# Softmax halves scaled back to back on GpSimd, the second sums ahead of the residual on VectorE, row places in PSUM

## What is computed

```python
x = x + xattn(layernorm(x), ctx)     # q, k, v, o with low-rank additions
                                     # softmax over 73 keys + softmax over 4 keys, 16 heads
h = layernorm(x)
top_logits, top_idx = top_k(h @ gate_w, 2)
top_w = softmax(top_logits)
x = x + sum_e combine[e] * (silu(h @ w1[e]) @ w2[e])
```

## Time and profile before

| | us |
|---|---|
| median of 3 runs | 716.13 (714.78 to 716.4) |
| the profiled execution | 715.26 |
| its span, first to last instruction | 713.5 |
| busy: TensorE / VectorE / GpSimd / ScalarE | 639.0 / 519.7 / 483.3 / 446.3 |
| mean granted TensorE clock | 0.988 of 2.4 GHz |

### The profile page before, as it was taken

How to read it: one execution, slowest core, us unless ns; L and a number is a source line. 1 busy time by engine, 2 the same in 40 slices (tenths; PEclk the granted TensorE clock), 3 DMA queues, 4 the chain that set the end, 5 groups by cost and what they waited for, 6 DMA issues and landing times. The chain is left out here.

```text
span 713.5 us, 22010 instructions
## 1 busy us (share of the span) xinstructions
PE 639.0 (90%) x7612; PEld 528.3 (74%) x7613; DVE 519.7 (73%) x1226; ACT 446.3 (63%) x768; POOL 483.3 (68%) x577
## 2 busy tenths in 40 slices
PE   6627799999999999999999999979999999999871
PEld 2215587788788888788788778757888888888751
DVE  3964679988988998898898898986577644445431
ACT  1436787778778778778778877854464454454330
POOL 3024645878878877977877887875677676556744
PEclk9999899999999999999999999999999999999997
DMA  8921111112111121111211211203769989655630
GB/s 263 322 79 21 32 34 52 48 45 68 47 55 57 47 62 50 59 53 48 75 36 48 80 32 48 78 16 77 119 124 136 133 119 139 92 82 87 86 48 6
DMA packets 87259, 55.31 MB, mean 78 GB/s; under 512 B 60784, under 2 KB 81520, under 8 KB 87216
## 3 DMA queue, kind: packets, MB, share of 16 engines
q1 hardware_dynamic: 73840, 37.41, 22.2%
q0 software_dynamic: 13376, 17.33, 13.4%
HBM read 20.27 MB, written 24.85 MB: 63 GB/s over the span
## 5 line engine op out<-in xcount | busy, mean ns | idle before, releaser
L527 POOL DMA_INDIRECT out_x<-pt_s,token_of x71 | 113.0, 1592 | 23.4 <-issue 21.4
L782 DVE TENSOR_TENSOR wq_s<-wk_s,wq_s 128x512 f16<-128x512 f32 (+1 forms) x78 | 51.5, 664 | 78.6 <-ACT wq_s L603 78.5
L598 ACT ACTIVATE wk_s<-ps 128x512 f32<-128x512 f32 (+1 forms) x78 | 43.5, 557 | 102.9 <-PE ps L1600 99.0
L1600 PE MATMUL ps<-ffnw,wq_s 128*128 x852 | 100.1, 273 | 6.3 <-DVE wq_s L782 4.8
L1600 PE MATMUL ps<-q_s,ffnw 128*128 128x256 f16 (+1 forms) x936 | 103.3, 264 | 2.1 <-issue 1.6
L959 POOL TENSOR_TENSOR prob<-prob,mx 128x1168 f32<-128x1168 f32 x64 | 77.6, 1233 | 37.6 <-DVE mx L1401 37.5
L1600 PEld LDWEIGHTS ps<-q_s,ffnw 128*128 x936 | 86.0, 98 | 15.2 <-issue 4.6
L1600 PEld LDWEIGHTS ps<-ffnw,wq_s 128*128 128x128 f16 x852 | 81.7, 98 | 19.8 <-issue 9.8
L1600 PE MATMUL ps<-wo_s,ot_s 128*128 128x256 f16 x768 | 89.4, 273 | 2.8 <-DVE ot_s L1338 2.8
L1600 PE MATMUL ps<-xt_s,wq_s 128*128 128x256 f16 x768 | 89.9, 279 | 1.9 <-DVE xt_s L1338 1.9
L1600 PEld LDWEIGHTS ps<-xt_s,wq_s 128*128 128x128 f16 x768 | 76.5, 100 | 13.0 <-issue 1.9
(11 more groups left out here) (232 smaller groups left out, 1176.0 us busy)
## 6 DMA issues: line engine op xcount, KB each, us to landing
wstage<-in_ffn_w SPq DMA_DIRECT2D x16, 512.0 KB, 3.6
x_sb<-in_x SPq DMA_DIRECT2D x4, 1024.0 KB, 10.8
out_x<-x_sb SPq DMA_DIRECT2D x16, 256.0 KB, 2.2
rows_dram<-wstage SPq DMA_DIRECT2D x8, 264.0 KB
out_x<-pt_s,token_of POOLq DMA_INDIRECT x71
pt_s<-in_wq SPq DMA_DIRECT2D x2, 512.0 KB, 4.4
pt_s<-in_wo SPq DMA_DIRECT2D x2, 512.0 KB, 8.4
rows_dram<-row_words,slot_i POOLq DMA_INDIRECT x64, 2.5
```

The lines of the kernel that those rows point to most:

```text
L527: pool.indirect_dma_start(out_rows, bass.IndirectOffsetOnAxis(ap=token_of[:, j % UNROLL, c:c + 1], axis=0), y_sb[:, j % UNROLL, c, :], Non ...
L598: act.activation(h32[:, half, 0:2 * n], h_ps(t, j, half)[:, 0:2 * n], ACT.Silu, scale=1 / WSCALE).then_inc(silu_done, 1)
L782: dve.tensor_tensor(hs[:, j % 2, 1, 2 * half:2 * half + 2, 0:n], h32[:, half, 0:2 * n].rearrange("p (f n) -> p f n", f=2), hs[:, j % 2, 0, ...
L1600: last = pe.matmul(o, lhs(a, n), rhs(c, n), start=(i == 0), stop=(i == len(steps) - 1))
```

## The change

Three things, in the streams of two engines. On GpSimd `normalise(b, 1)` follows `normalise(b, 0)` at once; `rstd_2(b - 1)` comes behind it, and then both scatters (in batch 15 the order stays as it was; in batch 1 only `rstd_2` changes its place). On VectorE `sums(b, 1)` comes ahead of `residual(b - 1)`, in every batch that has a residual. And `place` is no longer a tile in SBUF but 16 columns of the PSUM bank in which TensorE has left the ranks; `place` is written there by one VectorE instruction and read by the next but one, `picked`.

```diff
-        place = sb("place", [P, TPB, EXPERTS], F32)
...
                 normalise(b, 0)
-                if routed and not last:
-                    scatter(b - 2, 0)
-                if not first and not last:
+                normalise(b, 1)
+                if not first:
                     rstd_2(b - 1)
-                normalise(b, 1)
-                if last:
-                    rstd_2(b - 1)
+                if routed:
                     scatter(b - 2, 0)
                 if routed and not last:
                     scatter(b - 2, 1)
...
-                c.step(dve.tensor_tensor(place[:], rank, next_row[:].unsqueeze(1).to_broadcast([P, TPB, EXPERTS]),
+                place = rank_bank(b)[:, 4 * EXPERTS:6 * EXPERTS].rearrange("p (t e) -> p t e", t=TPB)
+                c.step(dve.tensor_tensor(place, rank, next_row[:].unsqueeze(1).to_broadcast([P, TPB, EXPERTS]),
                                          ALU.add))
...
-                    picked[:], picks[:], place[:].unsqueeze(1).to_broadcast([P, TOPK, TPB, EXPERTS]), ALU.mult))
+                    picked[:], picks[:], place.unsqueeze(1).to_broadcast([P, TOPK, TPB, EXPERTS]), ALU.mult))
...
+                sums(b, 1)
                 if not first:
                     residual(b - 1)
-                sums(b, 1)
```

## The result

| | before | after |
|---|---|---|
| median, us | 716.15 (714.78 to 716.4) | 724.94 (721.87 to 727.25) |
| ratio of the runs | | 1.0121, 95% interval 1.0089 to 1.0153 |
| the profiled execution / its span | 715.26 / 713.5 | 725.31 / 723.5 |
| one loop batch, scores to scores | 26.19 | 26.74 |

The changed kernel is 8.8 us slower; the forecast was +7.9 and 724.0.

A forecast was written before the change was run, and what follows sets the result against it. TensorE was fullest, with two nearly equally late chains, GpSimd's and VectorE's, ahead of attend. Loop +8.3 (13 x 0.64), batch 1 +0.8 and last batch -1.2 made +7.9 on the median 716.13: 724.0 us, range 716.0 to 729.0.

The forecast's parts named there:

- The two chains: Loop batch: GpSimd's normalise(b, 1) and VectorE's pt chain run side by side towards attend, the second almost as late.
- The loop: Batches 2 to 14: attend(b, 0) starts 0.64 us later in each, 13 x 0.64 = +8.3 us.
- VectorE slip: Loop: sums(b, 1), put first, wait for ScalarE's exp; everything from q(b + 1, 2) on slips 0.51 us.
- ScalarE hold: Loop: later rstd_2 delays ScalarE's normalise_2 and pt(b, 2), so VectorE's third pt_s waits another 0.42 us.
- 0.33 less 0.04 of cover: Loop: pt(b, 4) ended 0.33 us ahead of attend(b, 0) before; forecast to end 0.04 ahead (273.35, 273.39).
- Rival 2: Loop: ScalarE not held by the later rstd_2, only VectorE's slip counts, 0.23 a batch; 718.4 us, chance 0.15.
- Batch 1: No GpSimd wait to win there; it pays both slips, 0.51 and some 0.3: +0.8 us.
- The last batch: Batch 15: picked freed by place in PSUM, perhaps the count too, so maxima(15, 1) comes earlier: -1.2 us.
- rival 3: Last batch: place in PSUM doesn't free picked, residual precedes the transposes: +0.6 instead of -1.2; 725.8 us, chance 0.07.
- 1: Loop: GpSimd's wait is the limit and VectorE's order costs nothing, -0.28 a batch; 711.3 us, chance 0.11.
- 4: Loop: scatters in one row and the wstage load behind them reach ScalarE, 0.95 a batch; 728.1 us, chance 0.08.
- 5: Whole kernel: the halves of rivals 1 and 2 meet near 716.1 us; chance 0.07.

The follow-up runs named there:

- e5: The changed kernel with ScalarE's normalise_2 moved behind pt(b, 2) and pt(b, 3): 720.98 us, 26.48 a loop batch.
- e3: The kernel before with place in PSUM alone, both engines' orders as before: 714.31 us, 26.10 a loop batch.
- e6: The changed kernel with batch 15's tile count and scan moved from ahead of maxima(15, 1) to behind the attention: 724.53 us.
- e4: The kernel before with place in PSUM and GpSimd's rstd_2 between the two normalise, both scatters behind; VectorE's order unchanged: 710.62 us.
- e8: e4 with tile count and scan behind the attention, and GpSimd's low part of the expert weights in two halves, one earlier: 708.78 us.
- e1: The kernel before with GpSimd's new order alone, VectorE's order and place as before: 739.81 us, 27.87 a loop batch.
- e2: The kernel before with VectorE's new order alone, sums ahead of the residual: 724.04 us, 26.61 a loop batch.

## Why the prediction came out right, step by step

**The two chains.** Right, in place and sign: each row that was to show it is there (0.82 at `new_keys`, 0.43 for exp, 0.76 for `rstd_2`, no wait for `prob`, a gap ahead of `attend`); two are smaller than forecast, the gap ahead of `attend` (0.30, not 0.6) and the wait of the third pt_s (0.17, not 0.4).

**The loop, +0.64 a batch forecast, +0.55 measured.** The sum was made of a VectorE slip of 0.51, a ScalarE hold of 0.42, and 0.33 less 0.04 of cover. In the rows, the sums start where the sum had them (263.27 + 4.40), but the pair of sums and residual takes 3.54 instead of 3.45, so q(b + 1, 2) slips 0.60; the step from the first pt_s to the group of `pt(b, 4)` takes 3.38 instead of 3.18, and `pt(b, 4)` ends at 277.65, 0.83 late, where the sum had 0.93. The mis-sized term is ScalarE's hold, 0.20 in these rows and 0.26 by e5. Its lag behind `rstd_2` was taken at today's 0.23 and is 0.14 (273.27 to 273.41), inside the bound that the prediction gave (0.05); and VectorE, itself later by 0.60, met ScalarE later, so less of the hold was a wait. Rival 2 had the price without the hold nearly right, 0.23 a batch, as e5 shows (0.29), though in the changed kernel the hold is there.

**Batch 1, +0.8.** Measured +0.81, and by the forecast's two terms: the first pt_s comes 0.53 later behind the batch's scores (forecast 0.51), and `pt(b, 4)` another 0.29 (forecast some 0.3).

**The last batch, -1.2 forecast, -0.04 measured.** The step that failed. That `picked` is freed was right (0.18). Wrong was to give VectorE the whole wait back. GpSimd's work there, shift(15, 0) and `add_bias`, is waited for by whichever VectorE instruction with two inputs in SBUF comes next: before, `picked` and the count's comparison (1.41 and 1.27), after, the count and the scan (1.19 and 0.82). The prediction saw that the count is "held by GpSimd likewise" and yet counted it as gain. Each held instruction ends with the GpSimd instruction beside it: the count at 475.17 and the first of the two of shift(15, 0) at 475.15, the scan at 476.73 and `add_bias` at 476.70. e3 shows what place alone wins here, 0.55, and e6 that another 1.1 lies in these instructions. The Trainium skill, "SBUF — State Buffer", section "SBUF: two separate sides", gives the lock that would do this, held for the whole instruction by the side that starts first; the rows agree, down to an instruction of 128x8 that takes 1.19 us. Besides, the residual that the prediction charged with 0.2 at the values holds the first transposes: 15.97 behind the scores instead of 15.19. That is the price that rival 3 named (+0.6). The second half's transposes, which waited 1.36 for GpSimd before, then follow sooner, and the last `attend` ends where it did, 24.1 behind the first scores in both. So the two terms of this sum are place in PSUM, -0.55 by e3, and the residual behind the sums, the 0.51 by which the last batch of the changed kernel is longer than e3's.

**The total.** 8.3 + 0.8 - 1.2 = 7.9 was forecast; the traces have 6.87 + 0.81 - 0.04 = 7.64 in these places, and 2.3 more in work that the change doesn't touch. So the total fits better than its parts: the loop was put 1.4 too high and the last batch 1.2 too low, and that these cancel is luck.

**The rivals.** 1 (711.3, only the wait goes) falls with the 0.43 us of VectorE for exp; e4 shows that its price was real, -0.33 a batch, if VectorE's order is left alone. 3 falls with `picked` at 0.18. 4 (the load reaches ScalarE, and the batch pays for it) falls with the changed kernel's own rows and with e8: the load reaches ScalarE and stops in the cover of 0.7. 5 (716.1) falls with the measured time.

**Open.** What lets the clock fall in the last batch of e1, e2, e4 and e5: in e4 TensorE had stood idle 1.92 us ahead of its transposes, but in the kernel before it stands idle 1.98 us at the same place and keeps 1.00. And whether e4's last batch is as long in its other executions: only one of each kernel is profiled, so that all differences in the last batch rest on one trace each.

## What to carry to other kernels

A wait that one engine's order shows need not be a loss: what stands ahead of the waiting step may be filling the time until its input comes. Lay the streams of the two engines side by side and put the consumer's steps in the order in which the producer finishes them (e4), instead of turning both orders round. And when an instruction of one engine is freed from waiting for another engine's instruction, ask which one behind it will meet the same wait.

## What the runs showed of the hardware beyond what was expected

- VectorE wrote `place`, 128x16 floats, to PSUM in 0.18 us (e3) and to SBUF in 0.17 (before), and the product `picked` with one operand in PSUM ran in 0.18 beside the same GpSimd instruction beside which it took 1.83 with both in SBUF.
- The four scatters in one row take 0.97 to 1.04 us with 0.30 of issue between them (e4), as those in two pairs do.
- The mean granted clock of the last batch is 1.00 in some kernels and 0.91 to 0.95 in others with the same work on TensorE.
